# Second products of the shared expert two steps behind the first, with a third buffer

## The reference, cut to what matters

```
x = x + tanh(g0) * cosine_attention(layernorm(x), ctx)      # 4096 tokens, width 256
h = layernorm(x)
shared = (silu(h @ w1) * (h @ w2)) @ w3                      # hidden width 1024
s = sigmoid(h @ router_w);  top 2 of 16 experts by s + bias
routed = sum over the 2 chosen e: s[e] * ((silu(h @ w1[e]) * (h @ w2[e])) @ w3[e])   # hidden width 256
x = x + tanh(g1) * (shared + routed)
```

## Time and profile before

| what | value |
|---|---|
| median of three runs | 597.67 us (597.29 to 598.88) |
| the profiled execution, its own time | 600.83 us |
| its span in the profile | 598.7 us |
| mean granted clock of TensorE | 0.971 of full |
| TensorE busy | 550.9 us (92%) |
| VectorE, ScalarE, GpSimd busy | 362.7, 243.5, 273.7 us |
| bytes moved by DMA | 74.25 MB, mean 124 GB/s |

### The profile page before, as it was taken

The page is one execution under the profiler, slowest core; times in us unless marked ns, Lnnn a source line. Parts: engine busy times, 40 slices in busy tenths (PEclk is TensorE's granted clock), DMA queues, the critical chain, the costliest instruction groups (busy, mean ns, idle before and its releaser), DMA issues.

```text
span 598.7 us, 11199 instructions
## 1 busy us (share of the span) xinstructions
PE 550.9 (92%) x3410; PEld 351.6 (59%) x3410; DVE 362.7 (61%) x845; ACT 243.5 (41%) x541; POOL 273.7 (46%) x264
## 2 busy tenths in 40 slices
PE   4899899889899999598999999999999989879797
PEld 2567676555555566255666666666666555445454
DVE  2426887777877675356556556655665456454755
ACT  3435666652265554244343334333433323222322
POOL 3002675434387877733334333433340255637560
PEclk9879999999999999889999999999999999979899
DMA  8999353356151110021333333333442133624342
GB/s 236 316 376 358 125 175 142 142 194 211 36 159 36 55 37 0 2 73 37 111 114 111 107 113 117 109 107 110 111 111 78 54 108 86 193 72 133 99 138 71
DMA packets 54561, 74.25 MB, mean 124 GB/s; under 512 B 8256, under 2 KB 44544, under 8 KB 54512
## 3 DMA queue, kind: packets, MB, share of 16 engines
q1 hardware_dynamic: 44992, 52.67, 26.7%
q0 software_dynamic: 8944, 18.83, 11.9%
q10 hardware_dynamic: 576, 2.10, 1.1%
HBM read 50.56 MB, written 23.01 MB: 123 GB/s over the span
## 4 chain that ended last, share of the span: by engine, by line
PE 73%; DVE 11%; issue 6%; DMA 3%; POOL 3%; SPq 2%; ACT 2%; DVEq 0%; POOLq 0%; ACTq 0%
PE bank L1385 22%; PE bank L1468 17%; PE bank L1406 12%; PE bank L1488 9%; PE bank L1477 3%; PE bank L1457 3%; DMA WR<-in_ctx_t 2%; PE bank L1223 2%; POOL X L495 1%; PE bank L1250 1%; DVE STAGE L870 1%; DVE GS L1068 1%; DVE X L1040 1%; DMA xrow<-STAGE 1%; PE bank L1212 1%
## 5 line engine op out<-in xcount | busy, mean ns | idle before, releaser
L1385 PE MATMUL bank<-XTC,WS 128*128 128x512 f16 x768 | 180.3, 384 | 0.6 <-issue 0.5
L544 POOL DMA_INDIRECT ROWS<-xrow,idx x79 | 76.2, 964 | 118.9 <-PE bank L1457 113.8
L1385 PEld LDWEIGHTS bank<-XTC,WS 128*128 128x128 f16 x768 | 76.0, 99 | 81.8 <-issue 7.4
L1406 PE MATMUL bank<-WS,GS 128*128 128x256 f16 x768 | 98.5, 280 | 25.6 <-DVE GS L1068 14.0
L1468 PE MATMUL bank<-WR,XTB 128*128 x474 | 115.3, 379 | 0.6 <-issue 0.6
L1406 PEld LDWEIGHTS bank<-WS,GS 128*128 128x128 f16 x768 | 74.6, 100 | 53.8 <-DVE GS L1068 20.4
L561 POOL DMA_INDIRECT ROWS<-yrow,posi x64 | 65.4, 1021 | 67.4 <-DVE X L1052 29.6
L1062 DVE SCALAR_TENSOR_TENSOR G<-bank,SIL 128x512 f32<-128x512 f32 x63 | 43.5, 690 | 77.7 <-ACT SIL L698 57.4
L527 POOL DMA_INDIRECT slot_token<-tokid,sloti x64 | 74.6, 1165 | 23.6 <-issue 19.2
L698 ACT ACTIVATE SIL<-bank 128x512 f32<-128x512 f32 x63 | 37.6, 596 | 110.8 <-PE bank L1385 77.0
L1138 DVE SCALAR_TENSOR_TENSOR G<-bank,SIL 128x256 f32<-128x256 f32 x79 | 33.6, 425 | 76.0 <-ACT SIL L756 75.9
(11 more groups left out here) (156 smaller groups left out, 631.7 us busy)
## 6 DMA issues: line engine op xcount, KB each, us to landing
yrow<-ROWS SPq DMA_DIRECT2D x79, 128.0 KB
WR<-in_routed_w SPq DMA_DIRECT2D x39, 256.0 KB, 5.7
X<-in_x SPq DMA_DIRECT2D x4, 1024.0 KB, 12.6
xrow<-STAGE SPq DMA_DIRECT2D x8, 512.0 KB, 2.9
xtd<-STAGE SPq DMA_DIRECT2D x8, 512.0 KB, 2.6
out<-X SPq DMA_DIRECT2D x7, 512.0 KB
WR<-in_ctx_t SPq DMA_DIRECT2D x4, 768.0 KB, 10.2
WR<-in_shared_w SPq DMA_DIRECT2D x3, 1024.0 KB, 14.5
```

The lines of the kernel that those rows point to most:

```text
L544: pool.indirect_dma_start(out=XG[:, u, :], out_offset=None, in_=xrow, in_offset=bass.IndirectOffsetOnAxis(ap=idx[:, b:b + 1].bitcast(U32), ...
L1385: last = pe.matmul(acc[:, :], WS[:, wx, at:at + P], XTC[:, u, xx, k, :], start=(k == 0 and m == 0), stop=(k == KD - 1 and m == 2))
L1406: last = pe.matmul(acc, GS[:, a, gx, i * P:(i + 1) * P], WS[:, wx, at:at + D], start=(n in (NSE, n - j) and m == 0 and i % 2 == 0), stop=( ...
```

## The change

- The second products of step n - 2, not n - 1, follow the first products of step n (late_rows). At the seams late_rows(NSE - 2), late_rows(NSE - 1) and late_rows(NC * J - 2) are written out.
- A third buffer for the rounded part and the remainder: GATED[n % 3]. Its two halves lie in the memory of wv and wt, attention weights that are no longer used then; wt is allocated with 128 partitions for it. Rounding waits for s_y of n - 3.
- Start of the shared steps: first products 0, 1 (whole) and 2 run before the transposes of chunk 7, and 3 right after; gating 0 moves between the statistics and the deviations of chunk 7 on VectorE. ScalarE loads its table twice more there (Sqrt and Silu around deviation) and does silu 2 and 3 with their roundings before the sigmoid.
- VectorE's hand-written order of routing and gatings: gatings run further ahead; remainders 9, 10 and 11 and add_shared(0) move ahead of table_slots; block_words moves to step 14. ranks moves from step 5 to step 7 on TensorE, words from 9 to 13.
- Weight cuts start at step 13 with 2 and 1 a step, not at step 10 with 2, 1, 1.
- add_shared moves from slice 0 to slice 1 of the next chunk. In the combination steps the remainder stands ahead of the routed additions.
- GpSimd's SEL and RE products move from behind remainder 3 to behind remainder 6. Gating waits for the own engine's remainder of n - 2 where GpSimd's does not stand there.

```diff
+        GATED = ((GS[:, 0, 0, :], GS[:, 0, 1, :]), (GS[:, 1, 0, :], GS[:, 1, 1, :]),
+                 (wv[:, :, :].rearrange("p k h -> p (k h)").bitcast(F16),
+                  wt_all[:, :, :].rearrange("p k h -> p (k h)").bitcast(F16)))
...
-        CUTS = [0] * (J + 2) + [2, 1, 1] * 6 + [1] * 8
+        CUTS = [0] * (J + 5) + [2, 1] * 9 + [1] * 5
...
-                if n == 3:
+                hi, lo = GATED[n % 3]
+                pool.tensor_tensor(lo, G[:, n % 2, :], hi, ALU.subtract).then_inc(s_glo0, 1)
+                if n == 6:
...
-                if not first:
-                    act.wait_ge(s_y, n - 1)
-                act.activation(GS[:, a, 0, :], G[:, a, :], ACT.Copy).then_inc(s_ghi, 1)
+                if n >= 3:
+                    act.wait_ge(s_y, n - 2)
+                act.activation(GATED[n % 3][0], G[:, a, :], ACT.Copy).then_inc(s_ghi, 1)
...
             silu(0, 0, True)
-            hidden_hi(0, 0, True)
+            act.preload_act_table(ACT.Sqrt)
+            deviation(LAST)
+            act.preload_act_table(ACT.Silu)
             logits(LAST - 1, bank[6][:, 0:P])
+            silu(1, 1, True)
+            hidden_hi(0, 0)
+            hidden_hi(1, 1)
             lag(LAST)
-            silu(1, 1, True)
-            hidden_hi(1, 1, True)
+            silu(2, 2)
             logits(LAST, bank[6][:, P:2 * P])
+            hidden_hi(2, 2)
+            silu(3, 3)
+            hidden_hi(3, 3)
...
                 if pool is not None:
                     dve.wait_ge(s_glo0, pool)
+                elif not first:
+                    dve.wait_ge(s_glo, n - 1 if n - 2 < POOL_FROM else n - 1 - (POOL_TO - POOL_FROM))
...
-            gate_hidden(7, 1, pool=4)
+            gate_hidden(9, 1, pool=6)
+            hidden_lo(9, 1)
+            add_shared(0)
+            gate_hidden(10, 0, pool=7)
             slots_of_all(INCB)
+            hidden_lo(10, 0)
             block_experts(ends)
-            gate_hidden(8, 0, pool=5)
-            add_shared(0)
+            gate_hidden(11, 1)
             slots_of_choice(0)
+            hidden_lo(11, 1)
             slots_of_choice(1)
             table_slots()
...
                 gate_hidden(n, n % J)
-                if n % J == 0:
+                if n % J == 1:
                     add_shared(n // J - 1, combined=2 * done)
+                hidden_lo(n, n % J)
                 for t in range(done, done + TILES.get(n, 0)):
-                    add_routed(t, t % 4, (t // 4 + 1) * 32, based(n // J - 1))
+                    add_routed(t, t % 4, (t // 4 + 1) * 32, based((n - 1) // J - 1))
                 done += TILES.get(n, 0)
-                hidden_lo(n, n % J)
...
+            def late_rows(n):
+
+                shared_rows(n, n % J, based(n // J - 1) if n % J == 0 and n > 0 else None)
...
                     hidden(n, c % 2, j, load=(c // 2 * 16 + 16) if j == 0 else None)
-                    if with_routing and n == 5:
+                    late_rows(n - 2)
+                    if with_routing and n == 7:
                         ranks()
-                    if with_routing and n == 9:
+                    if with_routing and n == 13:
                         words()
-                    shared_rows(n - 1, (n - 1) % J, based(c - 1) if j == 1 and c > 0 else None)
...
-            hidden(1, 0, 1, first=True, products=(0,))
+            hidden(1, 0, 1, first=True)
+            hidden(2, 0, 2)
+            router_rows(LAST - 1)
             transpose2(LAST)
-            hidden(1, 0, 1, first=True, products=(1,))
-            router_rows(LAST - 1)
-            hidden(2, 0, 2)
+            hidden(3, 0, 3)
             router(LAST, bank[6][:, P:2 * P])
             pe.wait_ge(x2t, 2 * NC)
-            shared_rows(0, 0)
+            late_rows(0)
             router_rows(LAST)
-            shared_rows(1, 1)
-            steps(3, NSE, with_routing=True)
+            late_rows(1)
+            steps(4, NSE, with_routing=True)
+            late_rows(NSE - 2)
...
             block_transpose(0, 0, 16)
-            shared_rows(NSE - 1, EX - 1)
+            late_rows(NSE - 1)
             block_transpose(1, 1, 16)
...
-            shared_rows(NSE, EX)
             steps(NSE + 2, NC * J)
+            late_rows(NC * J - 2)
```

More of the change, by code:

```diff
@@ L93, in flamingo_block @@
         wv = sb("wv", [P, KD, H], F32)
-        wt = sb("wt", [KT, 2, H], F32)
+        wt_all = sb("wt", [P, 2, H], F32)
+        wt = wt_all[0:KT]
         rw = sb("rw", [P, KD, 2 * E], F32)
@@ L730, in _ @@
             half = 0
-            for n in range(2, NSE):
+            for n in range(4, NSE):
                 silu(n, n % J)
@@ L1078, in routed_lo @@
                     .then_inc(w_lo, 1)
+            attend(LAST)
+            statistics2(LAST)
+            gate_hidden(0, 0, True)
+            deviations2(LAST)
+            normalise2(LAST)
+            gate_hidden(1, 1, True)
+            hidden_lo(0, 0)
+            hidden_lo(1, 1)
             prepare()
-            gate_hidden(0, 0, True)
-            hidden_lo(0, 0)
-            gate_hidden(1, 1, True)
-            hidden_lo(1, 1)
+            gate_hidden(2, 0)
+            gate_hidden(3, 1)
             selection_scores()
             choose(0)
-            gate_hidden(2, 0)
+            gate_hidden(4, 0, pool=1)
             choose_lowest(0)
             exclude_first()
-            gate_hidden(3, 1)
+            gate_hidden(5, 1, pool=2)
             choose(1)
+            gate_hidden(6, 0, pool=3)
             choose_lowest(1)
             dve.tensor_tensor(OHS, OH[0], OH[1], ALU.add).then_inc(ohs_ready, 1)
-            gate_hidden(4, 0, pool=1)
-            gate_hidden(5, 1, pool=2)
+            gate_hidden(7, 1, pool=4)
             take_totals()
@@ L1104, in _ @@
             ends = sum_experts(INCB)
-            gate_hidden(7, 1, pool=4)
+            gate_hidden(9, 1, pool=6)
+            hidden_lo(9, 1)
+            add_shared(0)
+            gate_hidden(10, 0, pool=7)
             slots_of_all(INCB)
+            hidden_lo(10, 0)
             block_experts(ends)
-            gate_hidden(8, 0, pool=5)
-            add_shared(0)
+            gate_hidden(11, 1)
             slots_of_choice(0)
+            hidden_lo(11, 1)
             slots_of_choice(1)
             table_slots()
-            gate_hidden(9, 1, pool=6)
-            hidden_lo(9, 1)
+            gate_hidden(12, 0)
             gates()
-            block_words()
+            hidden_lo(12, 0)
             half = 0
-            for n in range(POOL_TO + 1, NSE):
-                gate_hidden(n, n % J, pool=n - 1 - POOL_FROM if n < POOL_TO + 2 else None)
-                if n % J == 0:
+            for n in range(J + 5, NSE):
+                gate_hidden(n, n % J)
+                if n == J + 6:
+                    block_words()
+                if n % J == 1:
                     add_shared(n // J - 1)
```

28 lines of the change are left out of this document (14 added, 14 removed).

## The result

| | before | after |
|---|---|---|
| times of the executions, us | 597.67, 598.88, 597.29, 598.22 | 590.73, 622.59, 590.56, 608.5 |
| ratio | 1 | 0.9877 (95%: 0.9853 to 0.9901) |
| span of the profiled execution | 598.7 | 589.0 |

The change makes the kernel 1.2% faster: 597.94 x 0.9877 = 590.6 us. Forecast were 578.5 and a range of 569 to 590.

What follows compares the result with a forecast made beforehand. TensorE was taken as the bound, idle 25.6 us before the second products. Gains of 3.7 us before the routed blocks and 15.5 after, 19.2 together, gave 581.6 from 600.8, or 578.5 from the median 597.67; range 569 to 590.

Steps and rivals of the forecast that it cites:

- the late silu of 4.9 us then costs 1.2: Shared steps after the routed blocks: a signal may be 3.7 us late, before 1.0, so little of the delay remains.
- stretch B: Shared steps after the routed blocks, to the last second product: 15.5 of 18.4 us lost would be saved, bounds 5.6 and 18.4.
- only loosen it: VectorE after the routed blocks: remainder ahead of routed tiles and chunk sum one step later were claimed only to help; no size.
- the 3.7 of the gatings: First product n needs gating n - 2; the signal for it may be 3.7 us late, before the change 1.0.
- Rival 1: Late signals of stretch B stay, perhaps from transfers: B gives 5.6 us, in all 9.3, so 588.4 us; chance 0.17.
- Stretch A, TensorE: First product 0 to the routed blocks: TensorE's own work ends at 255.3 us; block transposes now start at 273.76.
- Stretch A, the table chain: Before the routed blocks: slots, scatters, table and row fetch become the bound; first rows land at 268.6 us, not 261.5.
- The term of +2.7 us for more contention: Scatters before the routed blocks: six more weight cuts fall among them, at 0.45 to 0.5 us each.
- rival 5: Each VectorE cut blocks a GpSimd scatter for its whole 0.96 us: transposes 15 us later, 593.5 us in all; chance 0.05.
- The low clock: At the routed blocks' start, after TensorE waits for fetched rows: 2.5 us charged, bounds 0 and 5.
- The sum: First product 0 to the routed blocks: 5.2 us gained, 1.0 more for second product 35, 2.5 charged for clock, giving 3.7.

Runs made afterwards that it cites:

- first comparison: The first measurement of the changed kernel against the kernel before (about 598 us), TensorE held back: ratio 0.9877.
- set 5: Follow-up set with the kernel before at 609.0 us, TensorE strongly held back; the unedited changed kernel took 643.4 us, ratio 1.0478.
- 16 scatters: Only tiles 0 to 7 scattered, 16 of 64 transfers; changed kernel 560.8 us in set 4, 584.1 in set 5; kernel before 575.5 in set 4.
- set 2: Follow-up set with the kernel before at 576.1 us, TensorE not held back; the unedited changed kernel took 572.1 us, ratio 0.9953.
- set 4: Follow-up set with the kernel before at 576.7 us, TensorE not held back; the unedited changed kernel took 576.5 us, ratio 0.9964.
- set 3: Follow-up set with the kernel before at 615.3 us, TensorE strongly held back; the unedited changed kernel took 643.9 us, ratio 1.0644.
- set 6: Follow-up set, kernel before at 640.4 us, TensorE strongly held back; changed kernel with 16 of 64 scatters and 8 of 64 gathers took 569.1 us.

## Why the prediction was wrong, step by step

- **The step that failed** is "the late silu of 4.9 us then costs 1.2, and the half clock after it mostly goes", with the 15.5 us of stretch B that follow. Measured in B: 122.4 - 118.7 = 3.7 us. Of the 18.4 us that I called stall or low clock, 13.5 (122.4 - 108.9) are there only when TensorE is held by GpSimd's transfers; the other 4.9 the change does take away. In the kernel after a held B costs 14 to 16 us over its work of 104.0, and with scatters and gathers cut nothing, in a set in which the kernel before is held.
- **The path that I left out** is the chunk sum, of which I wrote that it and the remainder's place "only loosen it". Second product 0 of a chunk overwrites the rows that the sum reads, and between second product 7 and it stands one first product, before the change and after it: 2.59 us for a sum of 1.66, so 0.9 of slack (estimated from the rows), not the 3.7 of the gatings. In the first comparison the sum waited 4.38 us for a late signal and TensorE 5.54 for the sum, then did twelve second matmuls in 2.71; before it was 5.56 and 2.74. In set 5, with 16 scatters, a late silu takes the same path, as the gating stands ahead of the sum on VectorE:

```profile
514.37 0.60 ACT L701 ACTIVATE SIL<-bank 128x512 f32<-128x512 f32 x1 [7.73 <-remote]
515.00 0.69 DVE L1075 SCALAR_TENSOR_TENSOR G<-bank,SIL 128x512 f32<-128x512 f32 x1 [6.64 <-ACT SIL L701]
515.61 1.65 DVE L1051 SCALAR_TENSOR_TENSOR X<-bank,tgs,X 128x256 f32<-128x256 f32 x4
517.41 2.72 PE L1432 MATMUL bank<-WS,GS 128*128 128x256 f16 x12 [6.93 <-DVE X L1051]
```

- **Rival 1** ("The late signals of B stay and cost what they do now, for instance because they come from the transfers") was the right one, in mechanism and nearly in size: B 5.6 against 3.7 measured, total 588.4 against 590.6. It had 0.17. What should have raised it stood in the rows: both events of the earlier trace rows lie in the gathers, and silu began almost 5 us after its product by the list with no instruction between that could have delayed it. No instruction explains that wait, so the order of the queues was a guess.
- **Stretch A, TensorE**: the walk is right. Transposes at 118.33 without a wait; 1.63 us (forecast 1.9) for add_shared(0); arrival 145.4 us after the start against 145.6, where TensorE is not held. But the base was not what I took it for: of the 167.9 us of the kernel before 12 were holding (156.0 without it).
- **Stretch A, the table chain**: that it becomes the bound is right where TensorE is not held, and 13 us of waiting were forecast against 7.8 and 10.4 (in the first comparison none, as TensorE came too late to wait). The slots came as forecast (first scatter 164.89). The term of +2.7 us for more contention, a mean of 1207 ns, was mis-sized: with all 32 cuts inside, the mean was 1128 ns in set 2 and 1168 in set 4, so the chain ended 3 to 5.5 us sooner after the start than forecast (153.4 and 156.0 against 158.9). The full lock of rival 5 would have shown as a longer mean, which it isn't.
- **The low clock** after that wait: transposes to first block product 3.1 us (264.76 - 261.62) in set 2 against 2.8 in the kernel that doesn't wait, and 0.6 more in the blocks (194.7 against 194.1). About 1 us, where I charged 2.5.
- **The sum** in A: forecast 3.7. In the first comparison 6.0, because there TensorE is held in both kernels and the wait for the rows lies under it; free of holding -0.6 to -3.4. In the first comparison the sign was right, for reasons that were not mine.
- So the change is worth 0.4 to 0.5% where TensorE is not held (4.9 us won in B, the loss in A), 1.2% in the first comparison, and it costs some 5% in set 5 (1.048) and about as much, less surely, in set 3.

Open: why the kernel after is held some 20 us earlier than the kernel before, which would make it the slower one there. A clue: in all seven held traces of sets 3, 5 and 6 whose stretch A is that of the kernel after, the first gap begins 21.5 us behind the first scatter, behind the same matmul; in the kernel before of set 6 it is 41.4 us. Open too: what on the chip sets the state (sets 2, 4 and 5 carry the same chip number, so the number alone doesn't tell); and whether the version with second product 35 ahead is better where TensorE is not held, as it ran twice in held sets only. How much of B's 4.9 us is lag and how much the chunk sum is not settled either: both undone ran in held sets only, where B took 126.0 against 118.4 (set 5) and 125.8 against 119.6 (set 3), so that the new order does save 6 to 8 us there; lag alone undone ran free of holding, but with the sum in a place that lag 1 can't bear.

## What to carry to other kernels

Before a late signal is put down to the order of the queues, look at what its sender did: if TensorE stands between single matmuls for "issue" while a receiver waits for "remote", more distance between producer and consumer leaves the cause as it is (here it bought 3.7 of 18.4 us). And count the slack of every path, the shared buffer's too, not of the tightest one that comes to mind. Ask then which other engine ran in just those stretches, and take its work away in one run; that costs one kernel and separates what rearranging can't. And measure a change of about one per cent in several sets: here the same pair gave 0.988, 0.995, 0.996, 1.064 and 1.048.

## What the runs showed of the hardware

A GpSimd that issues indirect transfers back to back, one each 1.27 us, can hold TensorE down to one instruction each 1.40 us, in a kernel that uses one core and with DMA busy only 5% of the time. It took 50 us of stretch A in the kernel before (206.0 in set 6 against 156.0) and 69 in the kernel after (arrival 214.3 in set 5 against 145.4). It shows in four of six sets, more or less from execution to execution, and not in two, where the same scatters cost TensorE nothing (arrival 145.4 with 64 and with 16). The row fetches in the routed blocks, 79 indirect transfers spread over 190 us, never did it: the blocks take 194.1 to 195.9 us in all traces, held or not. The granted clock doesn't announce it: TensorE falls behind while it is still granted 2.4 GHz (165 to 190 us above) and is at 1.2 only after its pauses. How the transfers reach TensorE was not found, nor whether it is GpSimd's issuing or the transfers themselves, which no run separates; a heavy DMA load is not needed, and zero shared weights change nothing.
